# Identity products at both ends of a transformer layer kernel, and a new order for the last sequence's FFN

## What is computed

```python
x = x + attn(layernorm(x))
x = x + ffn(layernorm(x))
# attn: q, k, v = layernorm per head of (x @ W + b); softmax(q @ k.T / sqrt(8)) @ v; then @ Wo + bo
# ffn:  down(silu(gate(x)) * up(x)), integer weights times 1/127
```

## Time and profile before

| what | value |
|---|---|
| time, median of 3 runs | 363.91 us (363.26 to 381.69) |
| profiled execution, its own time | 364.82 us |
| span of its trace | 363.0 us |
| PE busy | 334.7 us, 92% |
| ACT busy | 279.7 us, 77% |
| DVE busy | 228.8 us, 63% |
| POOL busy | 60.5 us, 17% |
| mean granted clock of TensorE | 0.972 of 2.4 GHz |

### The profile page before, as it was taken

The page is one execution under the profiler, slowest core; times in us unless marked ns, Lnnn a source line. Parts: engine busy times, 40 slices in busy tenths (PEclk is TensorE's granted clock), DMA queues, the critical chain, the costliest instruction groups (busy, mean ns, idle before and its releaser), DMA issues.

```text
span 363.0 us, 10058 instructions
## 1 busy us (share of the span) xinstructions
PE 334.7 (92%) x3887; PEld 145.6 (40%) x3887; DVE 228.8 (63%) x594; ACT 279.7 (77%) x323; POOL 60.5 (17%) x106
## 2 busy tenths in 40 slices
PE   7568999999999999999999999999999998999766
PEld 6462332352254424442345225442443233222455
DVE  4883778877648854986668764885456442423435
ACT  1516989989878987899888987898788988989301
POOL 6762100320012200320031001220022100200020
PEclk9876999999999999999999999999999999999969
DMA  3533104123013300322022301230022203000000
GB/s 79 172 109 117 32 2 145 64 93 112 0 57 123 104 17 2 116 89 84 0 87 87 116 0 50 96 116 0 0 89 91 86 2 118 0 3 2 31 0 29
DMA packets 22803, 22.84 MB, mean 63 GB/s; under 512 B 3184, under 2 KB 19696, under 8 KB 22768
## 3 DMA queue, kind: packets, MB, share of 16 engines
q1 hardware_dynamic: 21200, 21.36, 18.1%
q10 hardware_dynamic: 1568, 1.02, 0.9%
HBM read 13.45 MB, written 8.65 MB: 61 GB/s over the span
## 4 chain that ended last, share of the span: by engine, by line
PE 56%; ACT 23%; issue 11%; DVE 5%; DMA 2%; ACTq 1%; POOL 1%; POOLq 0%; DVEq 0%
PE oacc L858 21%; ACT probs L726 19%; PE side L788 15%; PE scores L844 10%; PE side L781 7%; ACT osb L692 2%; PE scores L945 1%; ACT qk_sq L696 1%; DMA wraw<-in_L_attn_Wv 1%; DVE x2n L1029 1%; DMA kst<-parts 1%; ACT th L687 1%; POOL rs L534 0%; ACTq L725 0%; ACTq L391 0%
## 5 line engine op out<-in xcount | busy, mean ns | idle before, releaser
L726 ACT ACTIVATE probs<-scores 128x1024 f32<-128x1024 f32 x256 | 248.1, 1030 | 44.1 <-PE scores L844 43.1
L858 PE MATMUL oacc<-probs,vaug 128*32 128x512 f32 x1024 | 138.4, 611 | 2.2 <-ACT osb L692 1.7
L844 PE MATMUL scores<-qst,kst 32*128 32x512 f16 x512 | 72.9, 387 | 10.6 <-ACT probs L726 6.1
L844 PEld LDWEIGHTS scores<-qst,kst 32*128 32x128 f16 x512 | 20.2, 91 | 80.5 <-ACT probs L726 61.7
L532 POOL TENSOR_SCALAR ve<-mv 128x4 f32<-128x4 f32 (+1 forms) x17 | 9.0, 527 | 241.9 <-DVE mv L1023 218.1
L858 PEld LDWEIGHTS oacc<-probs,vaug 128*32 128x32 f32 x1024 | 20.7, 108 | 32.3 <-issue 30.7
L788 PEld LDWEIGHTS side<-wqkv,xnT 128*32 128x32 f32 x768 | 22.0, 111 | 14.0 <-issue 13.9
L788 PE MATMUL side<-wqkv,xnT 128*32 128x128 f32 x768 | 25.3, 275 | 0.9 <-DVE xnT L1050 0.9
L1231 DVE TENSOR_TENSOR y<-side,x 128x512 f32<-128x512 f32 x7 | 4.8, 691 | 31.3 <-PE side L788 31.3
L1221 DVE TENSOR_TENSOR hT<-side,ga 128x512 f32<-128x512 f32 x23 | 15.8, 691 | 11.6 <-PE side L788 11.0
L788 PEld LDWEIGHTS side<-wdT,hT 128*32 128x32 f32 x672 | 18.9, 110 | 8.4 <-issue 6.8
(11 more groups left out here) (154 smaller groups left out, 350.9 us busy)
## 6 DMA issues: line engine op xcount, KB each, us to landing
parts_dram<-parts SPq DMA_DIRECT2D x15, 256.0 KB, 2.4
qst<-parts_dram SPq DMA_DIRECT2D x15, 256.0 KB, 2.8
kst<-parts_dram SPq DMA_DIRECT2D x15, 256.0 KB, 3.0
x_in<-in_L_attn_x SPq DMA_DIRECT2D x8, 256.0 KB, 2.8
x_res<-in_L_attn_x SPq DMA_DIRECT2D x8, 256.0 KB, 3.5
out_dram<-y SPq DMA_DIRECT2D x8, 256.0 KB, 2.1
parts_dram<-parts SPq DMA_DIRECT2D x15, 128.0 KB, 1.9
parts_dram<-shift_fill SPq DMA_DIRECT2D x2, 128.0 KB, 3.2
```

The lines of the kernel that those rows point to most:

```text
L726: act.activation(probs[:, kt, 2 * c:2 * c + 2, :], scores[:, 2 * c:2 * c + 2, :], ACT.Exp)\
L844: last = pe.matmul(scores[:, j, :], kst[r, g, kt * P:(kt + 1) * P], qst[r, g, :], start=True, stop=True)
L858: last = pe.matmul(oacc[STRIP * j:STRIP * (j + 1), :], vaug[:, kt, NG * g + j, :], probs[:, kt, j, :], start=first, stop=last_of_half)
```

## The change

It has five parts.

1. PE multiplies the identity by itself at six more places (`keep_warm(n, out)`: n products of 128 columns into a bank that is free there): 6 after the output bias product (`WARM_FIRST`), 4 in unit 0 of the first turn (`WARM_UNIT`), and in the tail 2 before the transposes of `osb`, 2 before those of `on`, 11 before those of x2n and 3 between its halves (`WARM_LAST`).
2. Both halves of the x2n transposes come ahead of all gate and up products. These go by tile of the hidden width: gate j of half 0 and half 1, then up j of both, for j = 0, 1, 2.
3. ACT copies the transposes to x2T (with the semaphore `last_x2T_done`), where DVE did. DVE's passes become ga 0, hT 0, ga 1, hT 1, ga 2, hT 2; before it was ga 0, ga 1, hT 0, ga 2, hT 1, hT 2.
4. The fourth tile of the down product goes to bank 3 of `scores` and not to bank 1.
5. y is signalled by halves. SP stores tiles 0 and 1, ACT issues the store of tiles 2 and 3 from its own queue; SP waits for both.

```diff
--- before.py
+++ after.py
@@ -60,6 +60,9 @@
 PLACES = [[(0, 0, 1, 2), (1, 0, 2, 2)], [(0, 2, 1, 1), (1, 1, 1, 1)]]
 WARM_UP = 18
 WARM_AGAIN = 12
+WARM_FIRST = 6
+WARM_UNIT = 4
+WARM_LAST = {"osb": 2, "on": 2, "x2n": 11, "x2T": 3}
 STACK_DMAS = 2
 PART_DMAS = sum(len(p) for p in PLACES)
 
@@ -344,6 +347,7 @@
         x2n_done = sem("x2n_done")
         x2T_filled = sem("x2T_filled")
         x2T_done = sem("x2T_done")
+        last_x2T_done = sem("last_x2T_done")
         g_filled = sem("g_filled")
         u_filled = sem("u_filled")
         tanh_done = sem("tanh_done")
@@ -372,7 +376,7 @@
         x2Ts = [side[:, 2, :], oacc[:, :]]
         last_gates = [scores[:, j, :] for j in range(NF)]
         last_ups = [scores[:, 3, :], side[:, 0, :], side[:, 1, :]]
-        last_downs = [oacc[:, 0:D], side[:, 2, 0:D], scores[:, 0, 0:D], scores[:, 1, 0:D]]
+        last_downs = [oacc[:, 0:D], side[:, 2, 0:D], scores[:, 0, 0:D], scores[:, 3, 0:D]]
         HALF_TILES = NT // 2
         half_cols = [slice(0, S // 2), slice(S // 2, S)]
         half_tiles = [range(0, HALF_TILES), range(HALF_TILES, NT)]
@@ -510,8 +514,9 @@
             turn(B - 3, "near")
             turn(B - 2, "near")
             turn(B - 1, "last")
-            store_out(B - 1)
-            sp.wait_ge(out_stored, 16 * B)
+            sp.wait_ge(y_done, B)
+            sp.dma_start(out_t[B - 1, :, 0:HALF_TILES, :], y[:, 0:HALF_TILES, :]).then_inc(out_stored, 16)
+            sp.wait_ge(out_stored, 16 * (B + 1))
             sp.wait_ge(parts_stored, 16 * PART_DMAS * B)
             with sp.If(needs_max > 0):
                 sp.wait_ge(shift_cleared, 16 * B)
@@ -747,15 +752,26 @@
             act.wait_ge(OT_filled, NO * (B - 1) + 1)
             for cols in half_cols:
                 act.activation(osb[:, cols], oacc[:, cols], ACT.Copy).then_inc(osb_done, 1)
+            for half, cols in enumerate(half_cols):
+                act.wait_ge(x2T_filled, B + half)
+                act.activation(x2T[:, cols], x2Ts[half][:, 0:S // 2], ACT.Copy).then_inc(last_x2T_done, 1)
             for j in range(NF):
                 tanh(B - 1, j, last_gates[j])
+            act.wait_ge(y_done, B + 1)
+            act.dma_start(out_t[B - 1, :, HALF_TILES:NT, :], y[:, HALF_TILES:NT, :]).then_inc(out_stored, 16)
 
 
         @block.tensor
         def _(pe):
             pe.wait_ge(filled, 3)
-            for _ in range(WARM_UP):
-                pe.matmul(scores[:, 3, 0:P], ident[:, :], ident[:, :], start=True, stop=True)
+
+            def keep_warm(n, out):
+
+                for _ in range(n):
+                    pe.matmul(out, ident[:, :], ident[:, :], start=True, stop=True)
+
+            keep_warm(WARM_UP, scores[:, 3, 0:P])
+
             def prepare_later_weights():
                 for m, w in enumerate((wg_f, wu_f, wd_f)):
                     pe.wait_ge(ints_floated, m + 1)
@@ -880,9 +896,9 @@
                     prepare_later_weights()
                 piece(name, turn_before, occupant_in_prologue(k))
             pe.wait_ge(wT_copied, 3)
-            for _ in range(WARM_AGAIN):
-                pe.matmul(scores[:, 3, 0:P], ident[:, :], ident[:, :], start=True, stop=True)
+            keep_warm(WARM_AGAIN, scores[:, 3, 0:P])
             output_bias_product()
+            keep_warm(WARM_FIRST, scores[:, 3, 0:P])
             pe.wait_ge(flag_ready, 1)
             needs_max = pe.value_load(flag[0:1, 0:1], min_val=0, max_val=1)
 
@@ -905,6 +921,8 @@
                     todo = [p for p in slots_of(phase).get(u, []) if p[0] in PHASES[phase]]
                     scores_of(i, u, 0)
                     scores_of(i, u, 1)
+                    if phase == "first" and u == 0:
+                        keep_warm(WARM_UNIT, side[:, 0, 0:P])
                     if phase == "first" and u == 1:
                         pe.wait_ge(bo2_done, 1)
                     if u >= 1 or phase != "first":
@@ -920,10 +938,12 @@
             turn(B - 1, "last")
             times_v(B, -1)
 
+            keep_warm(WARM_LAST["osb"], scores[:, 0, 0:P])
             pe.wait_ge(y_done, B - 1)
             for half, tiles in enumerate(half_tiles):
                 pe.wait_ge(osb_done, NO * (B - 1) + 2 + half)
                 transposes(OTs[half], lambda t: osb[:, t * P:(t + 1) * P], tiles).then_inc(OT_filled, 1)
+            keep_warm(WARM_LAST["on"], scores[:, 0, 0:P])
             for half, tiles in enumerate(half_tiles):
                 pe.wait_ge(on_done, NO * (B - 1) + 2 + half)
                 transposes(onTs[half], lambda t: on[:, t, :], tiles).then_inc(onT_filled, 1)
@@ -933,29 +953,29 @@
                     last = pe.matmul(Wos[half][:, k * D:(k + 1) * D], onT[:, t * P:(t + 1) * P], wo[:, :],
                                      start=True, stop=True)
                 last.then_inc(Wo_filled, 1)
-
-            def last_x2T(half):
-                tiles = half_tiles[half]
+            keep_warm(WARM_LAST["x2n"], scores[:, 1, 0:P])
+
+            for half, tiles in enumerate(half_tiles):
                 pe.wait_ge(x2n_done, NT * (B - 1) + tiles[-1] + 1)
                 transposes(x2Ts[half], lambda t: x2n[:, t, :], tiles).then_inc(x2T_filled, 1)
-
-            def last_products(half, banks, w, done):
+                if half == 0:
+                    keep_warm(WARM_LAST["x2T"], scores[:, 1, 0:P])
+
+            def last_product(bank, weights, half):
                 cols = half_cols[half]
-                for j in range(NF):
-                    last = pe.matmul(banks[j][:, cols], w[:, j, :], x2T[:, cols], start=True, stop=True)
-                    if half == 1:
-                        last.then_inc(done, 1)
-
-            last_x2T(0)
-
-            pe.wait_ge(x2T_done, B)
-            last_products(0, last_gates, wgT, g_filled)
-            last_x2T(1)
-            last_products(0, last_ups, wuT, u_filled)
-            pe.wait_ge(x2T_done, B + 1)
-            last_products(1, last_gates, wgT, g_filled)
-            last_products(1, last_ups, wuT, u_filled)
-
+                return pe.matmul(bank[:, cols], weights, x2T[:, cols], start=True, stop=True)
+
+            for j in range(NF):
+                for half in range(2):
+                    if j == 0:
+                        pe.wait_ge(last_x2T_done, half + 1)
+                    if j == 0 and half == 0:
+                        pe.wait_ge(x2_done, B + 1)
+                    last = last_product(last_gates[j], wgT[:, j, :], half)
+                last.then_inc(g_filled, 1)
+                for half in range(2):
+                    last = last_product(last_ups[j], wuT[:, j, :], half)
+                last.then_inc(u_filled, 1)
 
             for j in range(NF):
                 pe.wait_ge(h_done, NF * (B - 1) + j + 1)
@@ -1406,19 +1426,15 @@
                            half_tiles[half])
             for half in range(2):
                 norm_apply(B - 1, x2, x2n, mv2, rs2, rs2_done, x2n_done, half)
-            for half, cols in enumerate(half_cols):
-                dve.wait_ge(x2T_filled, B + half)
-                dve.tensor_copy(x2T[:, cols], x2Ts[half][:, 0:S // 2]).then_inc(x2T_done, 1)
-            silu(B - 1, 0, last_gates[0])
             for j in range(NF):
-                if j + 1 < NF:
-                    silu(B - 1, j + 1, last_gates[j + 1])
+                silu(B - 1, j, last_gates[j])
                 times_up(B - 1, j, last_ups[j])
             dve.wait_ge(out_stored, 16 * (B - 1))
             for t in range(NT):
                 dve.wait_ge(d_filled, B + t)
                 last = dve.tensor_tensor(out=y[:, t, :], in0=last_downs[t], in1=x2[:, t, :], op=ALU.add)
-            last.then_inc(y_done, 1)
+                if t % HALF_TILES == HALF_TILES - 1:
+                    last.then_inc(y_done, 1)
 
 
 INPUTS = ["L0_attn_x", "L0_attn_Wq", "L0_attn_bq", "L0_attn_Wk", "L0_attn_bk", "L0_attn_Wv", "L0_attn_bv",
```

## The result

The changed kernel took 359.58 us (median of 4 runs, 358.49 to 360.85), against 363.95 us for the kernel before (4 runs): a ratio of 0.9882, with a 95% interval of 0.9835 to 0.9929. That is 1.2% faster, and less than the 2% at which a verdict here says faster. The profiled execution took 358.53 us. One of the four runs of the kernel before (381.69 us) was in a slower state of the chip and does not count in the ratio.

What follows compares the result with a forecast made beforehand. With PE nine tenths busy or more in the middle, only the two ends, with their half-clock dips, could answer. Gains 2.6 + 3.4 + 0.2 = 6.2 us took the median of 363.91 to 357.7 us, range 356.2 to 361.8.

Steps and rivals of the forecast that it cites:

- Start: Before and in the first turn: ten identity products keep PE at full clock, chain 4.75 instead of 7.40 us; gain 2.6 us.
- Tail: Last sequence's FFN: identity products hold full clock, with new order, copies and bank; y complete earlier, gain 3.4 us.
- Output: End of the kernel: storing y in two transfers gains 0.2 us, from 0.5 gained to 0.2 lost.
- the load of the flag: In PE's queue behind the six products after the bias product: taken as zero cost, 0.5 us late as far end.
- ACT's copies: Tail: ACT copies x2T instead of DVE; nothing taken for the swap.
- does it stay up?: Start: whether the clock stays full past 28.86 us with PE busy 2.8 of 4.6 us; the weak step, other end zero gain.
- rival B: Start: clock falls at about 28.9 us nonetheless, only 3.6 us gained, 360.3 us; chance 0.25.
- No row of this kernel has so much with a fall behind it: Start: PE's new activity, 2.8 of 4.6 us, exceeds the 2.7 of 5.5 ahead of the tail's fall.
- C: Tail: clock falls anyway at about 349 to 350 us, leaving 2.8 us gained, 361.1 us; chance 0.08.
- E: Tail at half clock from the Wo products on, identity products in the way: slower, 365.5 us; chance 0.04.
- The rule on transposes: Skill's rule that transposes do not count as busy PE; the tail's four, 347 to 348.7 us, would then be pauses.
- D: Clock falls at both start and tail: only the output's 0.2 us is gained, 363.7 us; chance 0.05.

Runs made afterwards that it cites:

- first experiment: Kernel before with only the ten identity products of the start added (6 after the bias product, 4 in the first unit): 362.92 us, ratio 0.9978.
- the third: Changed kernel without its 18 identity products in the tail; order, copies and output kept: 361.06 us, ratio 0.9922.
- the two with the start filled: Changed kernel with more identity products in the start, 359.59 us; and with such filling as fewer, 384-column products, program length unchanged, 359.28 us.
- the kernel with more filling: Changed kernel with more identity products around the FFN weight transposes, after the bias product and in the second unit: 359.59 us, ratio 0.9879.
- the one with long products: Changed kernel with the start filled by 384-column identity products, its program as long as the changed kernel's: 359.28 us, ratio 0.9863.

## Why the prediction was right or wrong

The time of 357.7 us was 1.9 us too low and the range held it. The direction was right, and the change stayed within 2%, the case that had most of the chances. That it lies so near is in part luck: two of the four executions were at 358.5 and two at 360.7, and the median fell between them.

**The sum, for its own execution, was right.** 358.6 was forecast of the profiled one and 358.53 measured; that the execution profiled was one of the low ones is luck. Start: 2.6 forecast, 2.66 measured. Tail: 3.4 and 3.28. Output: 0.2 and 0.36. The order of the tail stood as worked out: DVE's hT in time, transposes waiting for x2n and not for identity products, and the load of the flag free. ACT's copies, taken at nothing, cost 0.3 us at the second gate product: the twelve products took 5.49 us and not 5.2.

**The step that failed is "does it stay up?"**, together with the way from the profiled execution to the median. I treated the forecast and rival B as two worlds of which one would turn out true, and weighed them by the share of PE's time. Both are true, in different executions of the same program: of the ten executions of the changed kernel four were at 0.990 (one dip), three at 0.985 or 0.986 and three at 0.981 (two). The dips do not begin at the same place each time: the first one began at 15.21, 16.83, 15.23, 15.73, 17.07, 16.94, 17.65, 15.82, 16.20 and 17.88 us in ten traces whose kernels are alike up to there. Of the six that have the ten products, two had the first dip at 15.23 and 15.82, and the second came all the same (28.89 and 29.48); in four it was at 16.83 to 17.88, and there was none behind it. The Trainium skill (TensorE: Matmul & The Clock Gate, Part 1) says that the chip's look at PE's activity runs freely and is not started by the kernel; these traces agree, with starts over 2.7 us for the same work. The runs do not separate this from PE's own work, which the first dip also moves: PE's pause before the first scores was 1.31 and 1.32 us in the two traces with a second dip, and 0.45 to 0.69 in the four without. So an edit that shortens a pause changes how often a dip comes, and the gain in the median is a gain per dip times the share of executions that it saves. For the start that is 0.7 us on the kernel before (first experiment) and about 1 us on the rest of the change (0.9919 against 0.989, with intervals that overlap), not 2.6.

**The comparison that carried it was wrong too.** "No row of this kernel has so much with a fall behind it" held only because few rows were at hand. The prediction counted on PE busy 2.8 of 4.6 us; the fall at 28.89 came with 3.0 of 4.6, and the one at 303.33 after 2.33 of 3.40 us, in pauses of at most 0.53. Busy time by record is not a safe measure of what holds the clock.

**The base was a heavy execution.** The traced kernel before had three full dips, and took 364.82; nearly half of its executions (27 of 57) had fewer. I took the 0.9 us between it and the median for scatter, and subtracted the full gain from the median. A kernel with two dips has less to lose.

**The rivals.** B happened, near its size (360.3 forecast; 360.9 to 361.2 for two dips, 360.5 to 360.6 and one of 359.73 for one and a half). C and E did not: no trace with the tail's products has a dip there. The rule on transposes that stood behind C was not tested, since the run meant for it also halved the filling; there, with transposes in place of the products, the clock did fall in the tail. D, that the change does nothing, did not happen in any execution. The change was split right between its parts, but that order and clock help each other (0.33 us) was only in the sum and not said.

**Of the expectations,** several more failed: the low group of the first experiment, the 363 us of the third, and the 357.6 us of the two with the start filled. The first dip was to cost 0.9 us, by the transposes of q and k. From their start to the first scores it is 8.39 to 8.46 us in ten traces that have the whole of it, and 7.93 and 8.04 in the two without a dip: 0.4 to 0.5 us (the two with a short one have 8.43 and 8.01), since the stacks' transfers end that stretch. The start of the first scores alone tells nothing of it: with the dip it goes from 26.77 to 27.62. And the kernel with more filling was to win, and lost more than that by the stop in its stream.

## What to carry to other kernels

Read the mean clock of every execution before you compare medians: with a span and a clock per run, "0.3 us by the store" and "two dips instead of three" come apart, and a median over few runs mixes them. Here dips came in some executions of one program and not in others, so price an edit against them as gain times frequency, and look at every sparse stretch of TensorE, not only at the idle ones that one trace shows. Look at the loop's first pass after each change of the program's length; here long products gave the filling without more instructions, and the stop did not come.

## What was not expected of the hardware

- Dips of 3.4 us beside those of 6.8 (15.73 to 19.15 us in the changed kernel without its start, 303.33 to 306.74 in the one with long products).
- The clock falls in a stretch with PE busy 2.33 of 3.40 us by record, where the work is scores of 32 rows and products into 32-column strips, and no pause is over 0.53 us.
- The same microsecond at half clock costs little in some places: the first dip covers 6.8 us and costs 0.4 to 0.5, since transfers end that stretch; the one in the tail costs 2.2 to 2.5, and the one in the first turn 2.7.
- Fifteen products of 32 columns, or seventeen of 128, added ahead of a loop bring a stop of 1.2 us in PE's weight loads in its first pass. PE goes on 2.4 to 2.5 us after a 16 KB transfer of instructions has started (102.74 to 105.19 and 103.16 to 105.58 us).
- A transpose of 128 x 128 float32 values is one record and takes half as long as the product with the identity (11 in 1.36 us against 22 records in 2.62).
